# The output bias of three attentions: a GpSimd addition to x, or one product that opens each weighted sum

## The reference, cut to what matters

```
z    = layernorm(x)
q    = z @ Wq;  k = ctx @ Wk;  v = ctx @ Wv          # 16, 8 and 16 heads of 64, 77 keys per batch
attn = softmax(q k^T / 8)                            # per head; the first one is masked
x    = x + concat_h(attn_h v_h) @ Wo + bo            # bo: 128 values, the output bias
```

## Time and profile before

| | |
|---|---|
| median of three runs | 2963.92 us (2962.83 to 2964.83) |
| the profiled execution's own time | 2967.87 us |
| its span on the core | 2966.0 us, mean granted clock 0.911 |
| busy | PE 2507.0 us (85%), PEld 2031.3, DVE 2031.9 (69%), ACT 1445.3, POOL 465.5 (16%) |
| chain that ended last | PE 66%, DVE 16%, issue 7%, ACT 7%, POOL 1% |
| GpSimd's bias addition in the three attentions | 48 of it, 61.4 us busy |
| the 64 tiles of a0, a1, a2 | about 91 to 708 us, 890 to 1205 us, 1528 to 2137 us |

### The profile page before, as it was taken

The page is one execution under the profiler, slowest core; times in us unless marked ns, Lnnn a source line. Parts: engine busy times, 40 slices in busy tenths (PEclk is TensorE's granted clock), DMA queues, the critical chain, the costliest instruction groups (busy, mean ns, idle before and its releaser), DMA issues.

```text
span 2966.0 us, 52168 instructions
## 1 busy us (share of the span) xinstructions
PE 2507.0 (85%) x15073; PEld 2031.3 (68%) x15074; DVE 2031.9 (69%) x4751; ACT 1445.3 (49%) x2793; POOL 465.5 (16%) x621
## 2 busy tenths in 40 slices
PE   7899999996989999314579999999759997689998
PEld 5777777774877777201367777777557885578887
DVE  3788888887647888779947777777864435655554
ACT  5555555552445555125555555556324433435554
POOL 1011111110431121220011011010001002202223
PEclk9999999997989999755789999999859998869999
DMA  7344443442014444100034444444200000110000
GB/s 194 103 127 121 136 119 110 120 127 57 0 49 114 125 113 132 34 0 0 6 114 137 129 134 136 136 129 130 74 0 0 0 0 4 40 48 8 14 14 22
DMA packets 439185, 226.84 MB, mean 76 GB/s; under 512 B 19318, under 2 KB 435464, under 8 KB 438984
## 3 DMA queue, kind: packets, MB, share of 16 engines
q1 hardware_dynamic: 439112, 225.94, 26.8%
HBM read 120.78 MB, written 105.12 MB: 76 GB/s over the span
## 4 chain that ended last, share of the span: by engine, by line
PE 66%; DVE 16%; issue 7%; ACT 7%; POOL 1%; DVEq 1%; DMA 1%; SPq 0%; POOLq 0%; ACTq 0%
PE ps_o L720 8%; PE ps_s L708 8%; PE ps_p L86 6%; PE ps_p L88 5%; PE ps_p L87 5%; PE ps_t L696 5%; ACT a_keys L807 3%; DVE a_sm L938 3%; PE ps_o L1123 2%; PE ps_t L1123 2%; PE ps_s L86 2%; PE ps_t L2360 2%; PE ps_o L2360 2%; ACT a_e L852 2%; PE ps_s L88 2%
## 5 line engine op out<-in xcount | busy, mean ns | idle before, releaser
L938 DVE TENSOR_REDUCE a_sm<-a_e 128x16 f32<-128x1232 f32 (+1 forms) x192 | 233.9, 1218 | 281.4 <-ACT a_e L852 275.0
L720 PEld LDWEIGHTS ps_o<-a_val,a_pt 128*128 128x128 f32 (+2 forms) x3200 | 389.3, 193 | 34.0 <-issue 11.2
L708 PE MATMUL ps_s<-a_keys,a_zt 128*128 128x308 f32 (+1 forms) x1024 | 375.3, 499 | 33.8 <-DVE a_e L930 30.8
L720 PE MATMUL ps_o<-a_val,a_pt 128*128 128x128 f32 (+2 forms) x3200 | 393.4, 277 | 10.5 <-ACT a_pt L844 6.2
L844 ACT ACTIVATE a_pt<-ps_t 128x512 f32<-128x512 f32 (+1 forms) x448 | 223.2, 504 | 281.0 <-PE ps_t L696 280.0
L807 ACT ACTIVATE a_keys<-ps_p 128x308 f32<-128x308 f32 x614 | 262.5, 429 | 93.7 <-PE ps_p L88 92.8
L708 PEld LDWEIGHTS ps_s<-a_keys,a_zt 128*128 128x128 f32 x1024 | 185.7, 192 | 168.3 <-issue 96.1
L696 PE MATMUL ps_t<-ident,a_e 128*128 128x128 f32 (+1 forms) x1600 | 261.9, 278 | 44.5 <-DVE a_e L946 35.2
L816 ACT ACTIVATE a_stage<-ps_p 128x512 f32<-128x512 f32 (+1 forms) x370 | 221.0, 597 | 127.3 <-PE ps_p L88 111.0
L852 ACT ACTIVATE a_e<-a_e 128x1232 f32<-128x1232 f32 (+1 forms) x192 | 203.3, 1059 | 132.1 <-DVE a_e L930 132.1
L86 PE MATMUL ps_p<-ct_hi,a_mt_hi 96*128 (+1 forms) x614 | 239.9, 391 | 8.5 <-ACT a_keys L807 2.8
(11 more groups left out here) (363 smaller groups left out, 5140.2 us busy)
## 6 DMA issues: line engine op xcount, KB each, us to landing
a_vals<-a_stage SPq DMA_DIRECT2D x160, 512.0 KB, 3.3
a_val<-a_vals SPq DMA_DIRECT2D x128, 576.0 KB
a_vals<-a_stage SPq DMA_DIRECT2D x40, 416.0 KB
a_val<-a_vals SPq DMA_DIRECT2D x64, 256.0 KB
a_val<-a_vals SPq DMA_DIRECT2D x128, 40.0 KB
x<-in_x_dram SPq DMA_DIRECT2D x8, 512.0 KB, 7.6
out_dram<-x SPq DMA_DIRECT2D x8, 512.0 KB, 3.2
a_val<-a_vals SPq DMA_DIRECT2D x64, 52.0 KB
```

The costliest lines, as they stand in the source:

```text
L708: eng.matmul(o, zt, keys[:, h0:h0 + nh, :], start=True, stop=True)\
L720: mm = eng.matmul(c.ps_o[:, (i % 2) * P:(i % 2 + 1) * P], self.pt[0:r, n, :], self.val[0:r, i % 2, n, :], start=(n == 0), stop=(n == self. ...
L938: eng.tensor_reduce(self.sm[:, :], e, AX.X, ALU.add).then_inc(st.sem, 1)
```

## The change

Instead of a GpSimd addition for every four tiles, each tile's weighted sum begins with one more product: a 128x128 stationary operand of ones by a 128x128 moving operand whose row 0 holds the bias rounded to fp32r, whose row 32 holds the rest of it, and whose other rows are zero. Each of the 128 output rows so receives the bias, and the chunks' products add to it. The residual on VectorE then brings it to x. Prepared once per attention: GpSimd clears the bias tile, SP waits for that and loads bo into rows 0 and 32, and VectorE makes the ones, the rounded rows and the rest. The order of the waits in `weighted_sum` changes too: TensorE waits for the free half of ps_o, issues the bias product, and only then waits for the loaded values.

```diff
@@ __init__
+        self.ones = sb(ctx, n("ones"), [P, P], F32R)
+        self.bias_rows = sb(ctx, n("bias_rows"), [P, P], F32R)
-        self.bias_loaded = cl("bias_loaded", 16)
+        self.bias_clear = cl("bias_clear", 1)
+        self.bias_loaded = cl("bias_loaded", 32)
+        self.bias_ready = cl("bias_ready", 3)
-        self.ln = LayerNorm(core, twice, self.bias)
+        self.ln = LayerNorm(core, twice)
@@ sync
-            eng.dma_start(self.bias[:, :], s["bo"].partition_broadcast(P)).then_inc(self.bias_loaded.sem, 16)
+        eng.wait_ge(self.bias_clear.sem, self.bias_clear.at(1))
+        for row in (0, self.LOW):                      # LOW = 32
+            eng.dma_start(self.bias[row:row + 1, :], s["bo"].unsqueeze(0)).then_inc(self.bias_loaded.sem, 16)
         if self.setup:
             self.setup.load_x(eng)
@@ weighted_sum
+        eng.wait_ge(self.res_done.sem, self.res_done.at(t))
+        eng.matmul(c.ps_o[:, (i % 2) * P:(i % 2 + 1) * P], self.ones[:, :], self.bias_rows[:, :],
+                   start=True, stop=False)
         eng.wait_ge(self.val_in[i % 2].sem, self.val_in[i % 2].at(32 * (self.WIN // 2 * w + i // 2 + 1)))
-        eng.wait_ge(self.res_done.sem, self.res_done.at(t))
...
-                            self.val[0:r, i % 2, n, :], start=(n == 0), stop=(n == self.chunks - 1))
+                            self.val[0:r, i % 2, n, :], start=False, stop=(n == self.chunks - 1))
@@ tensor, ahead of the first turn_z
+        eng.wait_ge(self.bias_ready.sem, self.bias_ready.at(3))
@@ vector, behind the split of the product weights, ahead of the first layer norm (in a0: of its wait for x)
+        eng.wait_ge(self.bias_loaded.sem, self.bias_loaded.at(32))
+        eng.tensor_scalar(self.ones[:, :], c.ident[:, :], 0.0, 1.0, ALU.mult, ALU.add).then_inc(self.bias_ready.sem, 1)
+        eng.tensor_copy(self.bias_rows[:, :], self.bias[:, :]).then_inc(self.bias_ready.sem, 1)
+        eng.wait_ge(self.bias_ready.sem, self.bias_ready.at(2))
+        low = slice(self.LOW, 2 * self.LOW)
+        eng.tensor_tensor(self.bias_rows[low], self.bias[low], self.bias_rows[low].bitcast(F32), ALU.subtract)\
+           .then_inc(self.bias_ready.sem, 1)
@@ vector, body
-                if k == 0:
-                    eng.wait_ge(self.ln.bias_added.sem, self.ln.bias_added.at(g + 1))
@@ gpsimd
+        eng.memset(self.bias[:, :], 0.0).then_inc(self.bias_clear.sem, 1)
         self.copy_window(eng, 0)
         self.ln.pool(eng, 0)
-        eng.wait_ge(self.bias_loaded.sem, self.bias_loaded.at(16))
-        self.ln.pool_bias(eng, 0)
...
                 self.ln.pool(eng, g)
-                self.ln.pool_bias(eng, g)
...
         self.ln.pool(eng, GROUPS - 1)
-        self.ln.pool_bias(eng, GROUPS - 1)
```

More of the change, by code:

```diff
@@ L445 @@
     PART = 8
+    LOW = 32
     def __init__(self, core, name, heads, wq, wk, wv, wo, bo, before, twice=False,
```

## The result

| | us |
|---|---|
| before, median of 5 runs | 2964.83 (2962.83 to 2967.35) |
| after, median of 5 runs | 2981.98 (2978.93 to 2982.76) |
| ratio, 95% interval | 1.0054 [1.0040, 1.0069] |
| forecast | 2978.4, range 2966 to 2996 |
| profiled execution, before and after | 2967.87 and 2980.68 (spans 2966.0 and 2978.5) |

A forecast was written before the change was run, and what follows sets the result against it. The prediction took TensorE as the busiest engine, with 130 of 192 weighted sums on the chain. At 0.1115 us each these add 14.5 us, all other terms 0, to the median 2963.92: 2978.4 us, range 2966 to 2996.

The forecast's parts named there:

- The added product: One more TensorE matmul per weighted sum, 192 in all: 0.1115 us each for the 130 on the chain, +14.5 us.
- The smaller price: The Trainium skill's figure of about 81 ns per pair of load and 128-column matmul on TensorE: 10.5 us in sum.
- The distance of the records: In a2, the first chunk's record 0.11 us behind the ones' product; near 0.06 or 0.22 would mean wrong.
- The bounds: Limits for the added product's price on TensorE: 0.054 us (7.0 us in all) and 0.223 us (29.0 us).
- The 62 that cost nothing: Weighted sums off the chain, where TensorE waits for VectorE: product absorbed, 0; without that cover, 6.9 us.
- smallest of the gaps read: TensorE's 0.32 us wait for VectorE in a0, into which even a product of 0.223 us was to fit.
- Order of the waits: New wait order in the weighted sum: gives and costs nothing while the half of ps_o is free, 0.
- GpSimd and VectorE lose work: 48 additions of 1.28 us leave GpSimd and VectorE's wait for them goes: taken as 0.
- the bound of -6.6 us: The most that ending the addition's slowdown of L946 in a1 could give: 0.41 us in each of 16 groups.
- The start and the preparation: Loads of x 10 us later and three VectorE instructions under 2.1 us, all hidden by the first projections: 0.
- Rival D: Start exposed: late loads of x make the first tile up to 3 us late, 2981 us; 55% together with the forecast.
- B: The added product stays in TensorE's shadow or chain slack, leaving 0 to 5.9 us: about 2967 us; 14%.
- A: The short fp32r product on TensorE goes at fp32's rate, 0.22 us each: +29.0 us, 2993 us; 25%.

The follow-up runs named there:

- e1: The kernel before, GpSimd's addition kept, with the added product on rows of zeros: 2980.92 against 2966.41 us, ratio 1.0059.
- e5: The changed kernel with the 128-column bias product behind the first chunk's product instead of ahead of it: 2979.47 us, a single run.
- e7: The changed kernel with the bias product behind the first chunk and 64 columns instead of 128: 2975.71 us, a single run.
- e8: The changed kernel with ones and bias rows in bf16 instead of fp32r: 2981.71 us, ratio 1.0051 to the kernel before.
- e2: The kernel before without GpSimd's addition, VectorE's wait for it or any product, so without the output bias: 2964.84 us, ratio 0.9998.
- e6: The changed kernel with the bias product in plain fp32 (two records, two loads): 2995.07 against 2967.34 us before, ratio 1.0090.
- e4: The kernel before with the bias in the last chunk's free rows, all 128 rows used, neither addition nor product: 2963.90 us, ratio 0.9997.

## Why the prediction was right

**The added product: right, 14.5 us forecast, 14.5 in the traces, 16.0 [11.9, 20.5] in the runs.** The price of one, forecast at 0.1115 us, is 0.113 behind a projection and 0.111 behind the scores. The count, 130 by shares, is 134 if the weighted sums on the chain of the kernel before are counted (37, 45 and 52). That 14.5 came out to the tenth is luck: by e1, e5 and e7 the same product costs 15.2 to 15.4 us. The windows bear out the split better than the whole attentions do: forecast were 0.5, 0.6 and 0.7 us per window, measured 0.55, 0.58 and 0.64, and eight of each are 14.2 us. Per attention, forecast were 3.9, 4.8 and 5.8 us, measured 3.9, 4.0 and 6.5, and over the four kernels with one fp32r product a0 lost 3.9 to 5.7, a1 4.0 to 5.5 and a2 5.6 to 6.5. The differences among the four lie at the ends of the attentions. The smaller price that the prediction set beside its own, by which the sum would be 10.5 us, is not what this pair took.

**The distance of the records: wrong in form.** The prediction expected the first chunk's record 0.11 us behind the product, and said it would be wrong if that were near 0.06. It is 0.06. The bounds had both numbers, and taken for itself the 0.06 would have said "lower bound, 7 us". But the record that opens 0.05 us early is 0.05 us longer, so its start alone doesn't give the cost. The step's mechanism, one more distance between loads, stands: chunk 0's load waits for the product's matmul, and e5, e7 and e8 cost no less. Its test should have been from the projection ahead to the line behind the sum, 2.46 and 2.57 us.

**The 62 that cost nothing: right in two of the three gaps read,** 0.32 to 0.21 and 0.65 to 0.55, and in their like: in the first seven windows of a0 and a2 every gap of 0.3 us or more behind a sum shrank by 0.10 to 0.12. It did not hold for the third kind: the gaps ahead of a1's scores went from 0.39 to between 0.36 and 0.39. Some of a1's products were absorbed all the same, since its window grew by five products of eight (0.58 us); TensorE's waits for ScalarE's copies of the probabilities ahead of a1's chunks fell from 6.2 to 3.7 us. And the prediction's "smallest of the gaps read" was not the smallest there is: a2 has seven of 0.04 us, which are gone after. The forecast survives this, because its count came from the chain and not from the gaps.

**Order of the waits: right but for the ends.** TensorE's product waits for VectorE's residual L962 six times, 11.2 us in all. At a0's end, where the kernel before had its gap of 2.89 us too, the product waits 2.85:
```profile
713.06 0.48 PE L722 MATMUL ps_o<-a_bias_rows,a_ones 128*128 128x128 f32 x1 [2.85 <-DVE x L962]
```

**GpSimd and VectorE lose work: right, 0.** e2 shows it directly, and the bound of -6.6 us was never reached. L956 has a mean of 0.80 us over its 64 in a1, as expected:
```profile
L956 DVE TENSOR_TENSOR a_e<-a_e,a_rs 128x616 f32<-128x616 f32 x64 | 51.2, 800 | 2.2
```

**The start and the preparation: right, 0.** x was asked for at 23.0 us (24.5 forecast) and was there at 40.5 (44 forecast). The steps took 0.2 to 0.3 us each. Rival D had no cost to show: e1, whose start is as before, loses as much.

**The other rivals.** B (in the shadow) falls with e1's interval, whose lower end is 1.0043. A was given 25%; e6 is what it would have been, 27.6 us in the attentions beside the 29.0 worked out for it.

## What to carry to other kernels

On an engine that holds the chain, a small instruction can cost its place in the queue and not its size: one more small product in a row of fp32 products with 128-column loads cost one distance between weight loads (0.11 us), with 64 columns as with 128, and no less in bf16 than in fp32r. Multiply it by the number of such products on the chain, which the share of their line gives, not by their count. Before moving work from an idle engine to a busy one, look for room in what the busy one already does: the last chunk's free rows carried the same bias for nothing, and even then relieving the idle engine bought nothing. To check a small cost, compare the period of a steady loop: the windows agree to 0.02 us where whole attentions differ by 1.5.

## What I had not expected of the hardware

- A record's start is no sure sign of a matmul's cost: behind a long matmul the next but one opened 0.06 us later and was 0.05 us longer (0.32 instead of 0.27).
- A chunk of 128 rows took no longer than one of 80: 2.23 us a sum in e4 as before.
- A shorter load did not open sooner: behind a projection the fp32r load of the product opened with it (1651.15), the bf16 load of 0.10 us only 0.23 us later (1645.35), and the sum took 0.02 us more.
